# A vision-transformer layer on one core: who takes the low half of the images, and the order of the work around it

## The reference, cut to what matters

```python
h = _L0_tok_ref(x, W_proj, b_proj)                       # patches @ W_proj
h = jnp.concatenate([broadcast(cls_tok), h], axis=1)     # 197 tokens
h = h + _L0_attn_ref(_layernorm(h), wq, wk, wv, wo, w_gate, w_up)
h = h + _L0_ffn_ref(_layernorm(h), gate_w, ..., w1, b1, w2, b2)
# attention, for each expert e and head:
scores = jnp.where(mask, (q @ k.T) * scale, NEG)
attn = jax.nn.softmax(scores); outs.append((attn @ v) @ wo[e].T)
fused = jnp.concatenate(outs, -1)
return silu(fused @ w_gate.T) * (fused @ w_up.T)
```

## Time and profile before

| what | value |
|---|---|
| median of 3 runs | 4490.32 us (4490.26 to 4491.34) |
| profiled execution, its own time | 4492.27 us |
| span of its trace | 4490.5 us |
| TensorE busy | 3808.7 us, 85% |
| VectorE busy | 3302.0 us, 74% |
| ScalarE busy | 2733.0 us, 61% |
| GpSimd busy | 1246.6 us, 28% |
| mean granted TensorE clock | 0.950 of full speed |

### The profile page before, as it was taken

One profiled execution on the slowest core, in us unless ns is written; L12 is line 12 of the kernel. 1 busy time (PEld: TensorE's weight loads), 2 busy tenths in 40 slices (PEclk: granted clock), 3 DMA queues, 4 the chain that ended last, 5 costly groups with the idle time before them and its releaser, 6 DMA issues. The chain is left out here.

```text
span 4490.5 us, 124442 instructions
## 1 busy us (share of the span) xinstructions
PE 3808.7 (85%) x45994; PEld 2986.4 (67%) x45994; DVE 3302.0 (74%) x8109; ACT 2733.0 (61%) x8257; POOL 1246.6 (28%) x2008
## 2 busy tenths in 40 slices
PE   3888888888888888888888888888888888886998
PEld 2766666666676766666666667666666666764776
DVE  4777777777777777777777777777777777775665
ACT  2666666666666666666666666666666666662333
POOL 0332222222223332222222223332222222231222
PEclk7999999999999999999999999999999999997999
DMA  5122222111121222221111121222221111215664
GB/s 183 43 53 54 54 54 50 50 44 39 47 52 48 50 54 54 54 52 50 48 35 49 49 50 50 51 54 54 54 51 50 45 39 48 51 47 178 208 209 156
DMA packets 251462, 298.89 MB, mean 67 GB/s; under 512 B 57273, under 2 KB 234019, under 8 KB 241362
## 3 DMA queue, kind: packets, MB, share of 16 engines
q1 hardware_dynamic: 232114, 262.59, 21.9%
q0 software_dynamic: 18912, 29.35, 2.0%
HBM read 123.50 MB, written 39.28 MB: 36 GB/s over the span
## 5 line engine op out<-in xcount | busy, mean ns | idle before, releaser
L965 ACT ACTIVATE p_s<-bank,smin 128x128 f32<-128x128 f32 (+1 forms) x4864 | 1446.2, 366 | 888.9 <-DVE smin L1094 875.2
L1094 DVE TENSOR_REDUCE smin<-bank 128x3 f32<-128x384 f32 (+1 forms) x1792 | 906.6, 506 | 511.2 <-PE bank L772 461.3
L787 PE MATMUL bank<-ident_s,p_s 128*128 128x128 f32 (+1 forms) x4864 | 864.5, 283 | 316.8 <-DVE pt_f L1100 252.4
L787 PEld LDWEIGHTS bank<-ident_s,p_s 128*128 128x128 f32 (+1 forms) x4864 | 562.4, 144 | 440.0 <-ACT p_s L965 212.3
L757 PE MATMUL bank<-masks_s,mask_id_s 128*128 128x384 f16 (+1 forms) x1792 | 569.1, 318 | 106.1 <-PEq L1151 95.9
L1009 POOL TENSOR_TENSOR w_s<-o_raw 128x192 f32<-128x192 f32 (+1 forms) x512 | 308.4, 602 | 944.6 <-DVE o_raw L1055 944.1
L1100 DVE TENSOR_TENSOR pt_f<-bank,pt_f 128x384 f16<-128x384 f32 x1024 | 556.8, 544 | 0.0
L957 ACT CAST pt_f<-bank 128x384 f16<-128x384 f32 x1024 | 503.2, 491 | 0.0
L1015 POOL TENSOR_TENSOR w_s<-w_s,o_rcp 128x192 f32<-128x192 f32 (+1 forms) x512 | 261.4, 511 | 677.4 <-DVE o_rcp L1062 617.7
L844 PE MATMUL bank<-wgu_s,w_s 128*128 128x384 f16 (+1 forms) x2304 | 410.8, 326 | 0.0
L254 PE MATMUL bank<-zt,wqkv_s 128*128 128x394 f16 x1980 | 367.5, 330 | 1.6 <-DVE zt L364 1.2
(11 more groups left out here) (131 smaller groups left out, 6532.6 us busy)
## 6 DMA issues: line engine op xcount, KB each, us to landing
stacks_f<-qt_f SPq DMA_DIRECT2D x771, 73.9 KB, 2.1
stacks_f<-kt_f SPq DMA_DIRECT2D x1542, 36.9 KB, 2.1
wx_t<-wx_d SPq DMA_DIRECT2D x36, 1344.0 KB
x_raw<-x_t_dram SPq DMA_DIRECT2D x34, 1182.0 KB, 5.7
rec_t<-rec_d SPq DMA_DIRECT2D x36, 582.0 KB, 3.9
v_f<-v_f SPq DMA_DIRECT2D x64, 194.9 KB
stacks_f<-w_dram SPq DMA_DIRECT2D x2, 1536.0 KB
wx_d<-w_s SPq DMA_DIRECT2D x8, 384.0 KB
```

The source lines that it names most:

```text
L787: mm = nc.tensor.transpose(turned[0:kn, j * rows:j * rows + rows], p_slot(u)[:, j * kn:j * kn + kn], ident_s[0:rows, 0:rows])
L965: ins = nc.scalar.activation(p_slot(s)[:, j * kn:j * kn + kn], bank[s % SR][0:rows, j * kn:j * kn + kn], ACT.Exp, scale=-1.0, bias=smin[0: ...
L1094: nc.vector.tensor_reduce(least, ps, AX_X, ALU.min).then_inc(S["min_ready"], 1)
```

## The change

Seven things change.

- The low half of the images goes from GpSimd to VectorE. In the loop it is taken in six pieces of 128 x 394, each after its ScalarE cast (`x_hi` counts these), in the second stretch of the turn before. In the prologue VectorE takes it in one piece. The waits for `x_lo` at TensorE's step 22 and at the image DMA go.
- Ten products of constants (`mask_id_s` times `masks_s`, 128 x 384 each, into bank 7, which nobody reads) follow the turn's last projection on TensorE.
- The first value product of each window (unit 0 and unit 4 of a group) is done one step later, just ahead of the second one (`products_at`).
- VectorE's copy `take_o` stands after the minimum and the low half in its step, not ahead of them.
- Moments and normalisation of the next images are spread: moments from steps 37, 39, 41, 43 to 31, 34, 38, 41; normalisation from two and two in steps 46 and 47 to one each in 43, 46, 48, 49; the turns from 48 and 52 to 50 and 53.
- The turns of the attention output come one step sooner (37, 40, 43).
- In the routing, `weigh` goes from step 16 to 17 and `choose` from 17 to 18; `count` stays in step 19.

```diff
+                dve.wait_ge(S["x_hi"], 1)
+                nc.vector.tensor_tensor(x_s[:, 1], x_raw, x_s[:, 0], ALU.subtract)
...
-        AT_LOGITS, AT_WEIGH, AT_CHOOSE, AT_COUNT, AT_PLACE, AT_RANK = 15, 16, 17, 19, 20, 21
+        AT_LOGITS, AT_WEIGH, AT_CHOOSE, AT_COUNT, AT_PLACE, AT_RANK = 15, 17, 18, 19, 20, 21
...
+        def products_at(s):
+            return [u for u in (s - LAG_PV - 1, s - LAG_PV) if 0 <= u < UNITS and s - u - LAG_PV == (u % PER in (0, 4))]
...
-                            sp.wait_ge(S["x_lo"], 1)
                             sp.dma_start(x_raw, x_t[(i + 2) % STEPS]).then_inc(x_in, 16)
...
-                                pe.wait_ge(S["x_lo"], 1)
...
+                    for n in range(BUSY):
+                        nc.tensor.matmul(bank[OT_BANK][:, 0:HU * 128], mask_id_s[:], masks_s[:, 0:HU * 128],
+                                         start=True, stop=True)
...
-                        nc.scalar.copy(x_s[:, 0, k], x_raw[:, k])
+                        nc.scalar.copy(x_s[:, 0, k], x_raw[:, k]).then_inc(S["x_hi"], 1)
...
-                    nc.gpsimd.tensor_tensor(x_s[:, 1], x_raw, x_s[:, 0], ALU.subtract).then_inc(S["x_lo"], 1)
...
+                        for k in GATE_CAST[tt]:
+                            dve.wait_ge(S["x_hi"], k + 1)
+                            nc.vector.tensor_tensor(x_s[:, 1, k], x_raw[:, k], x_s[:, 0, k], ALU.subtract)
```

More of the change, by code:

```diff
@@ L213, in vit_layer @@
             o_copied o_summed o_rcp_ready o_ready ot_mm ot_hi ot_lo gu_mm sig_ready dve_own h_moved
-            tail_ready lg_mm lg_read onehot_ready pos_mm pos_read pos_ready x_lo""".split()
+            tail_ready lg_mm lg_read onehot_ready pos_mm pos_read pos_ready x_hi""".split()
         S = {n: sem(n) for n in names}
@@ L591, in _ @@
                 act.wait_ge(S["patch_mm"], 4)
-                nc.scalar.copy(x_s[:, 0], x_raw)
+                nc.scalar.copy(x_s[:, 0], x_raw).then_inc(S["x_hi"], 1)
             @block.gpsimd
@@ L671, in vit_layer @@
         Z2_TURNS = {9: 0, 12: 1}
-        AT_LOGITS, AT_WEIGH, AT_CHOOSE, AT_COUNT, AT_PLACE, AT_RANK = 15, 16, 17, 19, 20, 21
+        AT_LOGITS, AT_WEIGH, AT_CHOOSE, AT_COUNT, AT_PLACE, AT_RANK = 15, 17, 18, 19, 20, 21
         PATCH_STEP, PATCH_GAP, PATCH_LAG, PATCH_RATE = 22, 2, 1, 2
-        OT_STEPS = {38: 0, 41: 1, 44: 2}
+        OT_STEPS = {37: 0, 40: 1, 43: 2}
         OT_HI, OT_LO = 1, 2
-        Z1_MOMENTS, Z1_NORMS, Z1_TURNS = {37: 0, 39: 1, 41: 2, 43: 3}, {46: (0, 1), 47: (2, 3)}, {48: 0, 52: 1}
-        GU_STEPS = {57: 0}
+        Z1_MOMENTS, Z1_NORMS = {31: 0, 34: 1, 38: 2, 41: 3}, {43: (0,), 46: (1,), 48: (2,), 49: (3,)}
+        Z1_TURNS = {50: 0, 53: 1}
+        GU_STEPS, BUSY = {57: 0}, 10
         GATE_PROJ = (range(NV + 3, NV + 4), range(NV + 4, NV + 6), range(NV + 6, NV + 7), range(NV + 7, NV + 8))
@@ L898, in _ @@
                             turn_p(s - LAG_T)
-                        if 0 <= s - LAG_PV < UNITS:
-                            times_v(s - LAG_PV)
+                        for u in products_at(s):
+                            times_v(u)
                         if s in OT_STEPS:
@@ L1084, in _ @@
                     for s in range(UNITS + LAG_LO):
-                        w = window_at(s, LAG_OC)
-                        if w is not None:
-                            take_o(w)
                         if s < UNITS:
@@ L1101, in _ @@
                                                     ).then_inc(S["pt_lo"], 1)
+                        w = window_at(s, LAG_OC)
+                        if w is not None:
+                            take_o(w)
                         w = window_at(s, LAG_OR)
@@ L1126, in _ @@
                         if s in Z1_MOMENTS:
-                            if Z1_MOMENTS[s] == 0:
-                                dve.wait_ge(S["embedded"], 2)
+                            dve.wait_ge(S["embedded"], Z1_MOMENTS[s] // 2 + 1)
                             moments(chain, h_next, Z1_MOMENTS[s])
```

## The result

| | before | after |
|---|---|---|
| median of the runs | 4490.29 us | 4274.15 us (4 runs, 4273.6 to 4280.6) |
| ratio to before | | 0.9522 (0.9506 to 0.9539) |
| profiled execution, its own time | 4492.27 us | 4274.41 us |
| span of its trace | 4490.5 us | 4272.6 us |
| mean granted TensorE clock | 0.950 | 0.979 |

The change is faster by 4.8%, 216 us. The forecast was 300 us and 4190 us. The time lies in the range (4115 to 4280 us), at its upper end, 84 us from the forecast. The example turn of after starts at 1852.43 us of the span, and the one behind it at 1969.14.

What follows compares the result with a forecast made beforehand. TensorE (85% busy) and VectorE (74%) were neither at their end; losses were a 5.3 us stall, TensorE's fallen clock and many short waits. Terms summed to 300.1 us off 4492.3, giving a predicted median of 4190 us, range 4115 to 4280.

Steps and rivals of the forecast that it cites:

- the first: Rival at the turn's end: the clock falls all the same and the ten products only cost; 4243 us, chance 0.15.
- the second: Rival: later value products and spread moments win nothing, as low-half waits grow by what copy waits shrink; 4276 us, chance 0.09.
- stall and slow stretch, steps 6 to 13: TensorE's 5.3 us wait behind held normalisations and the slow clock after it go; gain 6.4 us a turn.
- routing and the rest, 13 to 20: The later choose makes TensorE's count wait; cost 0.5 us a turn, between 0 and 0.8.
- patch steps, 20 to 34: Later value products and copy, where TensorE has hardly a wait; gain 0.4 us a turn.
- steps 34 to 55: VectorE's full stretch: later value products, moved copy and spread tables together gain 2.3 us a turn, bounds 0 and 4.
- drain: From the minimum of step 55 to the first gate product; the prediction's sum had no term for it.
- end of the turn: With the ten products TensorE is last at the barrier; cost 0.75 us a turn.
- clock at the start: The clock stays up after the shortened idle time, so step 0 is faster; gain 1.7 us in 31 turns.
- prologue, once: VectorE waits for the cast ending at 99.01, then subtracts in the open for 2.6 us; cost 3.8 us once.
- I take that it holds in most turns: At the turn's start: the clock stays up after about 1.95 us idle, with dense work ahead and behind; nought the other end.
- GpSimd's lock on the spread normalisations: Rival in steps 43 to 49: normalisations meet GpSimd divisions, at most 0.6 us each; up to 4267 us, chance 0.02.

Runs made afterwards that it cites:

- pool_early: Kernel before with GpSimd's whole subtraction of the images moved to be its first instruction of a turn; 4310.9 us, ratio 0.9598.
- no_products: Changed kernel with all value products in their old steps and the output bank's copy ahead of the minimum again; 4272.6 us, ratio 0.9510.
- tables_back: Changed kernel with the old tables for the next images' moments, normalisations and turns and the attention output's turns; 4346.0 us, ratio 0.9684.
- early_c: Kernel before with GpSimd's subtraction first, ten products and new tables, but normalisations in steps 43, 44, 46, 47 and turns in 48, 52; 4253.8 us.
- products_only: Kernel before with only the later value products and the copy moved behind minimum and low half; 4493.7 us, ratio 1.0006.
- xlo_only: Kernel before with only the images' subtraction moved from GpSimd to VectorE, in six pieces (one in the prologue); 4325.8 us, ratio 0.9636.
- busy0: Changed kernel without its ten products of constants; 4279.7 us, ratio 0.9526.
- early_c0: The kernel of early_c without the ten products of constants; 4227.5 us, ratio 0.9412.

## Why the prediction was right or wrong, point by point

The prediction's own bounds for its forecast were 4140 to 4250 us, and the time lies outside them. It lies in the range because that took in the first two rivals. What came of the first (the clock falls at the turn's end all the same, 4243 us) is 18 starts of 31; the time of the second (4276 us) was met, its cause only in part.

The sum of the prediction, term by term, for one turn with a fallen clock at its start:

| term | forecast | measured | 32 turns (or as stated) |
|---|---|---|---|
| stall and slow stretch, steps 6 to 13 | +6.4 | +6.04 | 11.5 us less |
| routing and the rest, 13 to 20 | -0.5 | -0.83 | 10.6 us less |
| patch steps, 20 to 34 | +0.4 | +0.23 | 5.4 us less |
| steps 34 to 55 | +2.3 | +2.24 | 1.9 us less |
| drain | 0 | -0.75 | 24.0 us less |
| end of the turn | -0.75 | -0.74 | 0 |
| clock at the start | +1.7 in 31 turns | +1.66 in 13 turns | 31.1 us less |
| prologue, once | -3.8 | -4.6 | 0.8 us less |
| behind the loop | 0 | +3.3 | 3.3 us more |

The last column adds up to 82 us, which is 300.1 less the 217.9 us by which the span fell. Two things of before stand in no row and nearly cancel: the one start at which its clock held already (1.7 us), and its first turn, which was 2.7 us longer than the others.

- **The stall**: right in cause and size. The normalisation was held by GpSimd's instruction (pool_early), and TensorE's clock behind it gave nearly what the hand count gave. The missing 0.2 us is the price of the later value products in that group (10.77 against 10.56 us in no_products).
- **The clock at the turn's end**: the step that failed is "I take that it holds in most turns". It held at 13 of 31, and 12 of them are the change's. I had the row that spoke against it, with the clock fallen after 2.2 us, and weighed it too low. This is the largest part of the miss.
- **The drain** was no term of the sum. The new tables put the last turn of the next images into step 53, and so its low half into step 55 on VectorE, ahead of the last low halves, for which TensorE has no other work left. Before, this low half (line 364) stands ahead of the last minimum. tables_back and early_c, with the turn in step 52, have 1.60 us there; all with step 53 have 2.35 or more. I had followed no steps behind 13. VectorE's timeline of after shows it; TensorE's next turn of probabilities waits 0.65 us for the last of these rows:

```profile
1938.42 0.54 DVE L1104 TENSOR_TENSOR pt_f<-bank,pt_f 128x384 f16<-128x384 f32 x1
...
1939.13 0.56 DVE L364 TENSOR_TENSOR zt<-bank,zt 64x394 f16<-64x394 f32 x1
1939.72 0.56 DVE L1104 TENSOR_TENSOR pt_f<-bank,pt_f 128x384 f16<-128x384 f32 x1
```

- **Steps 34 to 55**: the number is right by two errors that cancel. I ascribed 2.3 us to products and tables together. The tables won 2.8 us (no_products against before), and the later products took 0.56 of it.
- **Value products**: the rival "they win nothing, waits change names" was the truth for this part (products_only), but it had been tied to the tables, which did win, so its time of 4276 us was met for other reasons.
- **Routing**: alone it costs 0.48 us (no_products against xlo_only, steps 13 to 20; the tables and the ten products, in which the two differ too, lie in other steps), as forecast. The other 0.26 us of that group are the later products again.
- **End of the turn**: right. 0.74 us against 0.75. xlo_only shows 0.23 of it for the subtractions, busy0 0.52 for the ten products.
- **Prologue**: the subtraction took 2.62 us and started at the cast's end, but the cast itself started at 97.49 us instead of 96.86, and ended at 99.64. From ScalarE's and VectorE's timelines:

```profile
97.49 2.15 ACT L592 CAST x_s<-x_raw 128x2364 f16<-128x2364 f32 x1
...
99.68 2.62 DVE L616 TENSOR_TENSOR x_s<-x_raw,x_s 128x2364 f16<-128x2364 f32 x1 [1.48 <-ACT x_s L592]
```

- **Behind the loop** 3.3 us were won that no term held; I haven't looked for them.
- **GpSimd's lock on the spread normalisations**: none of the 132 into `z` took over 375 ns, so this rival cost nothing.

## What to carry to other kernels

An instruction that takes ten times its usual time in a trace may well be held and not slow: look which other engine has an instruction over the same time, and try first to move that one to where the two don't meet. Here this won 180 us with one line moved, where cutting it into pieces lost 23. A change in how often the clock holds can hide a cost or a gain of the same size (22 us here), so compare turns that start alike and count the others. When a dependent chain runs through several engines, a wait that is removed mostly comes back under another name; compare stages between fixed marks of the program, not lists of waits. Count the last steps of a pipeline on their own, since nothing is left there to cover a late instruction.

## What the runs showed of the hardware that I had not expected

- In a row of six GpSimd instructions VectorE's normalisation was held over the first five (4948 ns at most), nearly as long as by one instruction of the same work (5122 ns). It ended 0.12 us behind the fifth, and the next one, held for 0.98 us, 0.12 us behind the sixth.
- After the same idle time of 2.0 us TensorE's clock fell to the lower level at 18 starts and held at 13, in one execution. With ten more products ahead of it, it held at 26, and after 3.1 us it held at 2 of 31 (busy0) but at 11 of 31 in another kernel (early_c0). So the length of the idle time alone doesn't tell. Within after, the idle times were 1.96 to 2.05 us where the clock held and 1.96 to 2.03 us where it fell. What decides in a single turn I have not settled.
- The clock also fell where no idle time was long: in 11 of 31 turns of xlo_only in steps 41 to 48. In the turn shown the longest wait of TensorE was 1.10 us, and it was busy for 1.67 us of the 3 us from 1940, with the clock at 1.00; the next 3 us show 0.53.

```profile
1942.55 0.56 PE L817 MATMUL bank<-v_f,w_s 128*69 128x33 f16 x12 [1.10 <-DVE o_raw L1054]
```
